# One expert's weights loaded once, w2's load moved back in SyncE's order, and buffers chosen by a table: a decoder layer on one Trainium2 core

## What is computed

```python
logits = hidden_states @ router_w + router_b
probs = softmax(logits)
topw, topi = top_k(probs, 4); topw = topw / sum(topw)
# for each expert e of 16, with its combine weights ce:
hmid = gelu(x @ w1e + b1e)            # 256 -> 512
out = out + (hmid @ w2e + b2e) * ce   # 512 -> 256
x = layernorm(x + out)
```

## Time and profile before

| | before |
|---|---|
| median of 3 runs | 634.78 us |
| the profiled execution | 640.26 us, span of its instructions 638.3 us |
| mean granted clock of PE | 0.925 of full speed |
| busy, share of the span | PE 86%, DVE 67%, ACT 54%, POOL 45% |
| DMA | 124.37 MB, mean 195 GB/s |
| the expert loop | about 334 to 604 us |

### The profile page before, as it was taken

The page is one execution under the profiler, slowest core; times in us unless marked ns, Lnnn a source line. Parts: engine busy times, 40 slices in busy tenths (PEclk is TensorE's granted clock), DMA queues, the critical chain, the costliest instruction groups (busy, mean ns, idle before and its releaser), DMA issues.

```text
span 638.3 us, 14320 instructions
## 1 busy us (share of the span) xinstructions
PE 550.0 (86%) x4060; PEld 514.3 (81%) x4060; DVE 429.9 (67%) x1061; ACT 342.7 (54%) x627; POOL 288.2 (45%) x262
## 2 busy tenths in 40 slices
PE   6999999999789999985499899999999999899700
PEld 5978888888679988875368899999899999899700
DVE  2645555555357888885546788878787888778326
ACT  2433333333135666663307677777777777677504
POOL 5541111111101466666610466656766666567623
PEclk9999999999769999998558999999999999999955
DMA  8899999400000122212275988899999999989477
GB/s 278 306 398 396 398 396 396 140 0 1 0 1 2 44 76 83 79 70 87 100 277 182 248 233 243 228 231 243 254 249 248 227 249 247 238 229 245 51 183 237
DMA packets 91675, 124.37 MB, mean 195 GB/s; under 512 B 6624, under 2 KB 62832, under 8 KB 91648
## 3 DMA queue, kind: packets, MB, share of 16 engines
q1 hardware_dynamic: 73984, 102.31, 48.3%
q0 software_dynamic: 14592, 19.41, 15.8%
q10 hardware_dynamic: 3072, 2.33, 1.1%
HBM read 61.88 MB, written 62.14 MB: 194 GB/s over the span
## 4 chain that ended last, share of the span: by engine, by line
PE 44%; DMA 17%; issue 14%; DVE 13%; SPq 5%; ACT 4%; POOL 2%; DVEq 1%; ACTq 0%; POOLq 0%
PE ps L348 9%; PE ps L350 8%; PE ps L349 8%; DMA w1f<-in_L_ffn_w 8%; DMA xg<-expert_rows 3%; DVE w_l L1457 3%; DMA expert_sum<-yb,home_row 2%; PE ps L885 2%; PE ps L730 2%; DMA expert_rows<-xd,idx 2%; PE ps L819 2%; PE ps L793 2%; PE ps L803 2%; DVE w_h L1450 2%; SPq L393 1%
## 5 line engine op out<-in xcount | busy, mean ns | idle before, releaser
L564 POOL DMA_INDIRECT expert_sum<-yb,home_row x80 | 165.5, 2068 | 123.3 <-DVE home_row L1485 100.6
L348 PE MATMUL ps<-gT_h,w_h 128*128 128x256 f32 x320 | 95.2, 297 | 1.8 <-issue 1.3
L348 PE MATMUL ps<-w_h,h_h 128*128 128x256 f32 x320 | 90.8, 284 | 2.0 <-DVE h_l L1478 2.0
L349 PE MATMUL ps<-gT_l,w_h 128*128 128x256 f32 x320 | 91.9, 287 | 0.0
L350 PE MATMUL ps<-gT_h,w_l 128*128 128x256 f32 x320 | 91.8, 287 | 0.0
L349 PE MATMUL ps<-w_l,h_h 128*128 128x256 f32 x320 | 90.5, 283 | 0.0
L350 PE MATMUL ps<-w_h,h_l 128*128 128x256 f32 x320 | 90.5, 283 | 0.0
L1095 ACT ACTIVATE hf<-ps,b1s 128x256 f32<-128x256 f32 x160 | 62.9, 480 | 31.9 <-PE ps L350 31.7
L545 POOL DMA_INDIRECT expert_rows<-xd,idx x64 | 62.8, 981 | 32.9 <-issue 21.1
L1478 DVE TENSOR_TENSOR h_l<-hf,h_h 128x1024 fp32r<-128x1024 f32 x40 | 49.0, 1225 | 32.9 <-ACT h_h L1102 32.3
L348 PEld LDWEIGHTS ps<-gT_h,w_h 128*128 128x128 f32 x320 | 62.5, 195 | 2.4 <-issue 1.5
(11 more groups left out here) (239 smaller groups left out, 1383.2 us busy)
## 6 DMA issues: line engine op xcount, KB each, us to landing
expert_rows<-zeros SPq DMA_DIRECT2D x32, 1088.0 KB, 13.7
w1f<-in_L_ffn_w SPq DMA_DIRECT2D x40, 512.0 KB, 5.9
w2f<-in_L_ffn_w SPq DMA_DIRECT2D x40, 512.0 KB, 4.2
xg<-expert_rows SPq DMA_DIRECT2D x40, 272.0 KB, 4.3
total<-expert_sum SPq DMA_DIRECT2D x16, 256.0 KB, 6.2
expert_sum<-zeros SPq DMA_DIRECT2D x1, 2304.0 KB, 15.9
x_all<-in_x SPq DMA_DIRECT2D x8, 256.0 KB, 7.0
expert_sum<-x_all ACTq DMA_DIRECT2D x8, 256.0 KB, 5.1
```

The source lines that it names most:

```text
L348: pe.matmul(o, ah, bh, start=first, stop=False)
L349: pe.matmul(o, ah, bl, start=False, stop=False)
L564: pool.indirect_dma_start(out=sums[p], out_offset=bass.IndirectOffsetOnAxis(ap=home_row[:, p, c:c + 1], axis=0), in_=yb[:, p, c], in_offse ...
```

## The change

```diff
-            def step_place(t):
-                rx = sp.value_load(tab[0:1, ds(t, 1)], min_val=0, max_val=E * CAP)
-                re = sp.value_load(tab[1:2, ds(t, 1)], min_val=0, max_val=E - 1)
-                return rx, re
+            def place_of(t):
+                return sp.value_load(tab[0:1, ds(t, 1)], min_val=0, max_val=E * CAP)
+
+            def expert_of(t):
+                return sp.value_load(tab[1:2, ds(t, 1)], min_val=0, max_val=E - 1)
+
+            def half_of(t):
+                return sp.value_load(tab[HALF_OF:HALF_OF + 1, ds(t, 1)], min_val=0, max_val=1)
+
+            def fresh(t):
+                return sp.value_load(tab[FRESH:FRESH + 1, ds(t, 1)], min_val=0, max_val=1)
...
-            def load_weights(t, p, re):
+            def load_up(t, p):
+                re, rb, rn = expert_of(t), half_of(t), fresh(t)
                 sp.wait_ge(w1h, freed(t))
                 sp.wait_ge(w1l, freed(t))
-                sp.dma_start(w1f[:, p], w1_rows[ds(re * D, D), :].rearrange("(k p) h -> p k h", p=P)).then_inc(f_w1[p], 16)
+                sp.dma_start(w1f[:, ds(rb, 1)].rearrange("p b k h -> p (b k) h"), w1_rows[ds(re * D, D), :].rearrange("(k p) h -> p k h", p=P),
+                             cond=rn, bounds_check="skip_entire_dma").then_inc(f_w1[p], 16)
+
+            def load_down(t, p):
+                re, rb, rn = expert_of(t), half_of(t), fresh(t)
                 sp.wait_ge(w2h, freed(t))
                 sp.wait_ge(w2l, freed(t))
-                sp.dma_start(w2f[:, p], w2_rows[ds(re * I, I), :].rearrange("(j p) d -> p j d", j=KI)).then_inc(f_w2[p], 16)
+                sp.dma_start(w2f[:, ds(rb, 1)].rearrange("p b j d -> p (b j) d"), w2_rows[ds(re * I, I), :].rearrange("(j p) d -> p j d", j=KI),
+                             cond=rn, bounds_check="skip_entire_dma").then_inc(f_w2[p], 16)
...
-            places = [step_place(t) for t in range(2)]
-            load_weights(0, 0, places[0][1])
+            load_up(0, 0)
+            load_down(0, 0)
+            places = [place_of(t) for t in range(2)]
...
             def load_step(t, p, k):
-                if isinstance(t, int) and t < 2:
-                    if t == 1:
-                        load_weights(t, p, places[t][1])
-                    return
-                rx, re = step_place(t)
-                load_rows(t, p, rx)
-                load_weights(t, p, re)
+                if not (isinstance(t, int) and t < 2):
+                    load_rows(t, p, place_of(t))
+                if not (isinstance(t, int) and t == 0):
+                    load_up(t, p)
+
+            def load_down_step(t, p, k):
+                if not (isinstance(t, int) and t == 0):
+                    load_down(t, p)
...
-            pipeline_upto(sp, more, [(0, load_step)])
+            pipeline_upto(sp, more, [(0, load_step), (1, load_down_step)])
...
             def w2_high(t, p, k):
+                side = act.value_load(tab[HALF_OF:HALF_OF + 1, ds(t, 1)], min_val=0, max_val=1)
...
+            tstep(dve.tensor_scalar(turned[:], ntile[:], 0.0, -2.0, ALU.is_gt, ALU.mult))
+            tstep(dve.tensor_tensor(turns[:], past[:], turned[0:NSTEP], ALU.mult))
+            tstep(dve.tensor_scalar(turns[:], turns[:], 1.0, None, ALU.add))
+            tstep(dve.tensor_reduce(side[:], turns[:], AX.X, ALU.mult))
+            tstep(dve.tensor_scalar(tabf[:, 2:3], side[:], -0.5, 0.5, ALU.mult, ALU.add))
+            tstep(dve.tensor_tensor(tabf[:, 3:4], sid[:], st[:], ALU.is_equal))
...
             def split_up(t, p, k):
+                side = dve.value_load(tab[HALF_OF:HALF_OF + 1, ds(t, 1)], min_val=0, max_val=1)
...
             def w2_low(t, p, k):
+                side = dve.value_load(tab[HALF_OF:HALF_OF + 1, ds(t, 1)], min_val=0, max_val=1)
```

More of the change, by code:

```diff
@@ L42 @@
 POOL_SETUP = 23
-TABLE_STEPS = 18
+TABLE_STEPS = 24
+PLACE, EXPERT, HALF_OF, FRESH = 0, 1, 2, 3
 KEEP_OK, BV_OK, AL_OK, WVO_OK, VO_OK, TURNED_OK, KT_OK, SETUP_DVE = 2, 4, 5, 6, 8, 13, 14, 15
@@ L160, in decoder_layer @@
         xs = sb("xs", [P, 2, D])
-        tab = sb("tab", [2, NSTEP], I32)
+        tab = sb("tab", [4, NSTEP], I32)
         more_pairs = sb("more_pairs", [1, 1], I32)
@@ L276, in decoder_layer @@
         row = sbl("row", [NSTEP, 1])
-        tabf = sbl("tabf", [NSTEP, 2])
+        tabf = sbl("tabf", [NSTEP, 4])
+        turned = sbl("turned", [P, E])
+        turns = sbl("turns", [NSTEP, E])
+        side = sbl("side", [NSTEP, 1])
         begun = sbl("begun", [P, PAIRS_MOST])
@@ L415, in _ @@
             for t in range(2):
-                load_rows(t, t, places[t][0])
+                load_rows(t, t, places[t])
             def load_step(t, p, k):
-                if isinstance(t, int) and t < 2:
-                    if t == 1:
-                        load_weights(t, p, places[t][1])
-                    return
-                rx, re = step_place(t)
-                load_rows(t, p, rx)
-                load_weights(t, p, re)
+                if not (isinstance(t, int) and t < 2):
[5 more added lines that the diff above has]
+                    load_down(t, p)
             more = sp.value_load(more_pairs[0:1, 0:1], min_val=0, max_val=PAIRS_MOST - PAIRS_LEAST)
-            pipeline_upto(sp, more, [(0, load_step)])
+            pipeline_upto(sp, more, [(0, load_step), (1, load_down_step)])
             for p in range(2):
@@ L879, in _ @@
                     pe.wait_ge(tb_dve, TABLE_STEPS)
-                    pe.transpose(ps[0:2, 7, 0:NSTEP], tabf[:], ident[0:NSTEP, 0:NSTEP])
+                    pe.transpose(ps[0:4, 7, 0:NSTEP], tabf[:], ident[0:NSTEP, 0:NSTEP])
                     pe.transpose(ps[0:E, 7, NSTEP:2 * NSTEP], stepe[:], ident[0:NSTEP, 0:NSTEP]).then_inc(tb_ps, 1)
@@ L1085, in w2_high @@
             def w2_high(t, p, k):
+                side = act.value_load(tab[HALF_OF:HALF_OF + 1, ds(t, 1)], min_val=0, max_val=1)
                 act.wait_ge(f_w2[p], 16 * k + 16)
                 act.wait_ge(yps, freed(t))
-                act.activation(w2_h[:, p], w2f[:, p], ACT.Copy).then_inc(w2h, 1)
+                act.activation(w2_h[:, p], w2f[:, ds(side, 1)].rearrange("p b j d -> p (b j) d"), ACT.Copy).then_inc(w2h, 1)
             def gelus(t, p, k):
@@ L1430, in _ @@
             dve.wait_ge(tb_ps, 1)
-            dve.tensor_copy(tab[:], ps[0:2, 7, 0:NSTEP]).then_inc(tb, 1)
+            dve.tensor_copy(tab[:], ps[0:4, 7, 0:NSTEP]).then_inc(tb, 1)
             dve.tensor_copy(stepeT[:], ps[0:E, 7, NSTEP:2 * NSTEP]).then_inc(tb, 1)
@@ L1447, in split_up @@
             def split_up(t, p, k):
+                side = dve.value_load(tab[HALF_OF:HALF_OF + 1, ds(t, 1)], min_val=0, max_val=1)
                 dve.wait_ge(f_w1[p], 16 * k + 16)
                 dve.wait_ge(hps, freed(t))
-                dve.tensor_copy(w1_h[:, p], w1f[:, p]).then_inc(w1h, 1)
+                raw = w1f[:, ds(side, 1)].rearrange("p b k h -> p (b k) h")
+                dve.tensor_copy(w1_h[:, p], raw).then_inc(w1h, 1)
                 dve.wait_ge(w1h, done(t))
-                dve.tensor_tensor(w1_l[:, p], w1f[:, p], f(w1_h[:, p]), ALU.subtract).then_inc(w1l, 1)
+                dve.tensor_tensor(w1_l[:, p], raw, f(w1_h[:, p]), ALU.subtract).then_inc(w1l, 1)
             def w2_low(t, p, k):
+                side = dve.value_load(tab[HALF_OF:HALF_OF + 1, ds(t, 1)], min_val=0, max_val=1)
                 dve.wait_ge(w2h, done(t))
                 dve.wait_ge(yps, freed(t))
-                dve.tensor_tensor(w2_l[:, p], w2f[:, p], f(w2_h[:, p]), ALU.subtract).then_inc(w2l, 1)
+                dve.tensor_tensor(w2_l[:, p], w2f[:, ds(side, 1)].rearrange("p b j d -> p (b j) d"), f(w2_h[:, p]), ALU.subtract).then_inc(w2l, 1)
             def home_in(t, p, k):
```

## The result

| | before | changed |
|---|---|---|
| median (runs) | 635.18 us (4; 634.44 to 640.97) | 656.85 us (4; 654.45 to 659.2) |
| ratio, 95% interval | | 1.0346 (1.0301 to 1.0390): slower |
| the profiled execution | 640.26 us, span 638.3 | 659.2 us, span 657.4 |
| moved by DMA | 124.37 MB | 99.22 MB |

The layer became 22 us slower although it moves 25 MB less. The forecast was 650 us, slower; the range was 630 to 664.

The account below looks back on a forecast made before the run. PE's pace is the floor now; SyncE's program order was to become the bound at 7.1 us a step. Over 37 steps +16.2, less 0.6, gives +15.6 us: 655.9 on the profiled execution, 650 us on the median, range 630 to 664.

Parts of the forecast that it names:

- SyncE as the new pace: Expert loop: SyncE's own program takes 7.1 us a step, above the present 6.64, and becomes the bound.
- Reads: SyncE's step: 7 table reads instead of 2; the five more add 3.30 us a step.
- Preparing the two conditional loads: SyncE's step: registers for buffer half and skip condition of each weight load add 0.18 to 0.54 us, taken as 0.35.
- Issues: SyncE's step: skipped loads' issue changes it by -0.44 to +0.22 us, taken as -0.25.
- The order's gain: w2's load one round later ends SyncE's wait for line 1457; alone it gives PE's floor, up to 15.5 us less.
- The sum: Step 39's `xg` goes out 16.2 us later, less 0.6 for its landing: +15.6 us on the profiled execution.
- the start: Before the loop: four more reads ahead of the first `xg` issue cost nothing, at worst 1 us.
- The last landing: End of the loop: skipped transfers shorten the last `xg` landing, 5.1 us now, by 0.6 us, once.
- Reads on DVE and ACT at no cost: Two reads a round on DVE, one on ACT, overlap the datapath; DVE's 5.9 us stays under 7.1, costing nothing.
- The table steps: Six more steps building the table, 1.2 us, hidden where DVE waits 2.80 us for PE.
- A: Rival, faster: SyncE's step stays at 6.2 us or less, the loop falls to PE's floor: 623 us, chance 0.15.
- C: Rival, slower still: PE idles 0.9 us a round, or DVE and ACT reads tie with SyncE: 665 us, chance 0.16.

Follow-up runs that it names:

- e9: The changed kernel with the first two row loads issued ahead of the first step's weight loads and their table reads: 651.93 us, ratio 1.034 to the kernel before.
- e2: The kernel before with w2's load one round later and unused reads added, 7 table reads a step on SyncE, nothing skipped: 629.36 us, ratio 1.002.
- e5: The kernel before with w2's load one round later and unused reads added, 9 table reads a step on SyncE, nothing skipped: 680.91 us, ratio 1.076.
- e8: The changed kernel, but the loop body's second round reuses load_up's three words for w2, 5.5 reads a step: 618.62 us, ratio 0.977 to the kernel before.
- e1: The kernel before with only w2's load moved one round later in SyncE's order, 3 reads a step, nothing skipped: 620.41 us, ratio 0.983.
- e6: The changed kernel without table reads on DVE and ACT, which pick buffers by parity; SyncE's program unchanged: 651.91 us, ratio 1.028 to the kernel before.
- e7: The changed kernel without table reads on DVE and ACT and with the flag 1 in every step, so no load is skipped: 662.12 us, ratio 1.046.
- e11: A second run of the changed kernel with load_up's words reused for w2 in the body's second round: 619.20 us, ratio 0.984 to the kernel before.
- e3: The changed kernel with expert, half and flag packed in one table word, 3 reads a step on SyncE: 619.83 us, ratio 0.984 to the kernel before.

## Why the prediction was right

**SyncE as the new pace: right.** The step said 7.1 us, the profile has 7.10. It hit by terms that nearly cancel, and the second decimal is luck: e9 ran the same loop at 6.99. Reads: 7 x 0.66 = 4.6 forecast, 4.69 measured. Preparing the two conditional loads: 0.35 more forecast, 0.46 measured (0.77 us for both, against 0.31). Issues: -0.25 forecast, -0.34 measured (0.52 for both weight loads, against 0.86). The rest of the step was put about 0.1 too high, the slow read counted twice that e2 laid bare. That a read's count is causal, and not only the sum, is shown by e2, e5 and e8 from both sides.

**The order's gain: right in mechanism.** Up to 15.5 us to PE's floor was the forecast. In the profiles e1 goes the full way, from 6.66 to 6.15 us between issues; on the medians it has 10 us.

**The sum: 15.6 us forecast, 19.1 in the profiles.** In them `xg` of step 39 is 19.75 us later. Of that 37 x 0.44 = 16.3 is the pace (forecast 16.2) and 3.5 is the start (forecast 0, at worst 1): **this is the term that was off**. Timelines of DVE, SyncE and PE in the changed kernel:

```profile
321.43 0.20 DVE L1458 CAST tab<-ps 4x48 int32<-4x48 f32 x1 [0.49 <-DVE more_pairs L1455]
326.75 0.41 SPq L416 DMA_DIRECT2D w1f<-in_L_ffn_w  x1
330.37 0.39 SPq L423 DMA_DIRECT2D w2f<-in_L_ffn_w  x1
333.16 1.05 SPq L410 DMA_DIRECT2D xg<-expert_rows  x2
337.86 1.97 PE L921 MATMUL ps<-ident,xg 128*128 128x128 f32 x8 [4.63 <-DMA xg<-expert_rows]
```

`xg` of step 0 stood behind eight table reads (four before) and two loads, and went out 7 us later than in the earlier trace rows, not 3.6. Round 0 opened at 337.86 instead of 334.38. But most of this lies in this one execution. e6, e7, e8 and e11 have the same program on SyncE up to here; e11's profile:

```profile
314.12 0.20 DVE L1462 CAST tab<-ps 4x48 int32<-4x48 f32 x1 [1.43 <-PE ps L904]
323.21 1.00 SPq L410 DMA_DIRECT2D xg<-expert_rows  x2
327.90 2.15 PE L925 MATMUL ps<-ident,xg 128*128 128x128 f32 x8 [1.78 <-DMA xg<-expert_rows]
```

From the start of the table's copy to `xg` it was 5.3 us before and 11.7 in the changed kernel's profile, but 9.1 in e11 and 8.7 to 9.7 in all four: 3.4 to 4.4 more, close to the forecast's 3.6. From the copy to round 0 it was 13.5 us before and 16.4 in the changed kernel, but 13.8, 14.0, 15.4 and 13.8 in e6, e7, e8 and e11, so 0.3 to 0.5 us more in three of them and 1.9 in one. The rest of the 3.5 is a copy 0.6 us later and over 2 us of records on SyncE that only this profile has (they are shown at the end). That is also why e9's repair of the start gains nothing that can be seen.

The last landing took 3.75 us instead of 5.1 (forecast -0.6, measured -1.35), and the tail was 0.7 longer. The medians are 21.7 us apart; the 2.6 beyond the profiles is within what single executions of these kernels differ by (the changed one: 654.45 to 659.2), and I do not assign it.

**Reads on DVE and ACT at no cost: right.** The first lies under `h_l`, the second shows 0.31 us of DVE idle before `w_l`:

```profile
459.15 0.69 DVE L1503 TENSOR_TENSOR gT_l<-ps,gT_h 128x512 fp32r<-128x512 f32 x1
460.16 1.23 DVE L1487 TENSOR_TENSOR w_l<-w2f,w_h 128x1024 fp32r<-128x1024 f32 x1 [0.31 <-issue]
```

e8 keeps PE full with them in place, and e6, without them, is no faster per step than e9 (6.98 against 6.99 us). **The table steps** stayed hidden in the profiles of e6, e7, e8, e9 and e11, but not in the changed kernel's own, where PE stood 0.90 us for the last of them:

```profile
321.08 0.20 PE L899 MATMUL ps<-ident,tabf 48*4 48x48 f32 x1 [0.90 <-DVE more_pairs L1455]
```

What I had not named: w2 now lands late in the steps that transfer it, and ACT waits 61.4 us for it. PE waits 20.3 us for `xg` and only 1.9 for `h_l` in the same stretch, so nearly all of it fell in PE's slack.

**Rivals.** A (the loop falls to PE's floor) is what e8 and e3 make of the change with 1.5 and 4 reads fewer: its condition, under 6.68 us of SyncE a step, was the right one; e2, at 6.55, is level with the kernel before. C did not happen: the granted clock was 0.97 to 1.00 over the windows of 50 us from 350 to 600 us. In windows of 10 us it was below 1.00 in two places, 0.93 and 0.90 from 470 to 490 us and 0.83 from 580 to 590 us, the last as low as in the earlier trace rows. A load's issue alone is short beside the load, 0.39 us against 3.87 from w1's issue at 462.12 to its landing. Three loads with their reads and preparations took 7.1 us of the sequencer.

## What to carry to other kernels

Count a DMA-issuing engine's program as a stage of the pipeline. An engine that mostly waits can become the bound by a few small instructions: SyncE waited 2.9 of 6.7 us a step, and five reads with what belongs to them used up more than that. Take its waits out, add the new instructions, and compare with the pace of the loop. A number read at run time costs that sequencer more than issuing the DMA that it steers (0.67 us against 0.38 here), so read it once and keep it, or pack several in one word. And split a change before judging it: here one half was worth -1.7%, and the other cost it all and 3.5% more.

## What the runs showed of the hardware

- A table read on SyncE takes 0.62 to 0.72 us with its checks, as a kernel's mean; its load proper takes 0.27 at the median but 0.5 to 0.7 now and then (19 of 81 in the kernel before). Reads follow each other with no overlap: 9 of them were 5.6 of 7.8 us (e5).
- A load skipped by its condition moved nothing and still raised its semaphore. The changed kernel moved 25.15 MB less, 48 loads of 512 KB, and DVE and ACT, which wait for the loads' counts in every step, made all 40 conversions of w1 and of w2. In e8's trace each of the 48 skipped loads has an update of its semaphore 0.06 to 0.09 us after its issue began. In the changed kernel's, w2's skipped issue of 464.83 is what ended ACT's wait: `w_h` began 0.19 us behind it, where behind the transferred load issued at 472.38 it began after 4.06 us.

```profile
465.02 1.06 ACT L1108 ACTIVATE w_h<-w2f 128x1024 fp32r x1 [0.37 <-DMA w2f<-in_L_ffn_w]
...
476.44 1.06 ACT L1108 ACTIVATE w_h<-w2f 128x1024 fp32r x1 [5.72 <-DMA w2f<-in_L_ffn_w]
```

- A skipped load's issue took 0.09 us at the median in e6, a transferred one's 0.38 in e7, over the loads between the `xg` issues of steps 10 and 38. The condition and the buffer address from a register added 0.23 us of preparation to a load (0.77 us for two, against 0.31), and as much in e7, where none is skipped.
- In the changed kernel's first reads SyncE's records stand 0.70 us apart several times in a row, with pieces of 0.02 us and less between them; later reads of the same lines show nothing of it, nor does any other profile here, e8's and e11's with the same instructions included. What it is stays open. It made up over 2 us of the start's 3.5.

```profile
322.50 0.31 SPq L402
322.81 0.70 issue
323.51 0.02 SPq L402
323.52 0.70 issue
324.23 0.01 SPq L402
324.25 0.69 issue
```
